# Weights fetched in column halves, eight PSUM banks for the first expert chunks, and a last stage with more buffers

## The chip, the cores and the metric

The kernel runs as one program on all 8 cores of one Trainium2 chip. Each core works on one of the 8 sequences of the batch and needs nothing from the others. The metric is the device time of the slowest core, in microseconds; lower is better.

## The reference

One transformer layer on x of shape 8 x 4096 x 1024 in float32: attention with a single head of width 1024, a residual and a layer norm, then an expert layer in which each of 64 expert slices picks one token out of every group of 16, again with residual and layer norm. Cut to what is computed:

```
qkv = x @ W_qkv + b_qkv;  q, k, v = split(qkv)
attn = softmax(q @ k.T / 32);  out = (attn @ v) @ W_out + b_out
x = layernorm(x + out)
logits = einsum(groups of 16 tokens, controller)        # 16 tokens x 64 slices
perm   = one-hot of the largest logit over the 16 tokens
sel    = the chosen token's row, for each group and slice
inner  = relu(sel @ f1[slice] + bias);  inter = inner @ f2[slice]
out    = inter handed back to the chosen tokens
x = layernorm(x + out)
```

## The kernel before, in words

Five engines run lists of instructions that Python writes out in order; each engine works through its own list strictly in order and waits on counters of the others. `wait` puts a wait in front of the next instruction of a list, `dma`, `mm`, `act` and `ve` append one instruction. So the order of the code is the order on each engine. All DMA starts from the list of SyncE (SP), ScalarE (ACT) or GpSimd (POOL). PSUM has eight banks, `bank(0)` to `bank(7)`; `bank_free[i]` holds the counter value at which bank i may be written again.

**The head.** Attention is reordered by algebra. AM = Wq Wk^T and W2 = Wv Wo are made first, with 128 matmuls each, then V' = x W2 (512 matmuls), then scores = x AM x^T. All weights and the transposed x come in as float32 in pieces of 512 KB: 16 for AM, 16 for W2, 32 for x, numbered as `feeds`. `feed(j)` (L176) starts the DMA of piece j into one of eight staging slots (slot j % 8, after the cast of piece j-8), and puts the cast to bf16 on VectorE (DVE) for even j and on ScalarE for odd j. `product` (L191) makes one half ("part") of AM or W2: four row blocks times two column halves fill all eight banks, and the sum runs over d = 0 to 7, where step d needs the d-th piece of both weight matrices. `evacuate` copies the eight banks out, four on DVE and four on ACT. Between AM and W2 stand small matmuls with the biases: 64 for `UB` (bank 0), 16 for the row constant `WC` (banks 1 and 2), and 16 for the output constant `CO` (banks 3 and 4) which read all of Wo. The V' loop (L267) makes 32 row blocks of 16 matmuls, each half evacuated by DVE with an addition of `CO`.

**The middle** (from some 217 to some 1230 us) is attention over 64 half rows; the change doesn't touch it.

**The expert stage** gathers chosen tokens and multiplies by f1 (until some 1374 us). Then comes a loop over j (L875): `product2(j, k)` multiplies by f2 into a pair of banks, `product2_out` copies the pair to one of two buffers `INP[j % 2]`, on DVE for even k while j < 3, on ACT otherwise; `swap(j-1)` (L665) is one transposing DVE instruction that needs all eight copies of the chunk before. From j = 3 on `combine(m)` (L687) adds the residual (read back from DRAM by `load_hr` into one of two buffers in `CB`) and hands expert outputs back to the tokens, in bank 4 + m % 4; `stats2`, `rstd2`, `shift2` and `finish2` make the layer norm and write y. A finished second half goes through one of two buffers in `WC` (L740), and SP stores it. Blocks 4(j-3) to 4(j-3)+3 are combined in iteration j, so iterations 16 to 19 hold only the end.

Of the kernel before, what the change touches and what calls it, by code (L numbers as in the profile page):

```python
# [49 lines left out]
def build_nc():  # L50
# [102 lines left out]
    d_id = dma(C, "id", IDT[:], ident_d)  # L153
    d_bo = dma(C, "bo", WC[:], bout_d)
    d_fb = dma(C, "fb", FBT[:], fbias_d)
    d_gl = dma(C, "gl", GLM[:], glmask_d)
    d_cb = dma(GP, "cb", CB[:], ctrl_d)
# [6 lines left out]
    for d in range(NC):
        feeds.append((wkt_d[d * 128:(d + 1) * 128, :], V[:, WK + d * 1024:WK + (d + 1) * 1024]))
        feeds.append((wqt_d[d * 128:(d + 1) * 128, :], V[:, WQ + d * 1024:WQ + (d + 1) * 1024]))
    for d in range(NC):
        feeds.append((wvt_d[d * 128:(d + 1) * 128, :], A[:, WV + d * 1024:WV + (d + 1) * 1024]))
        feeds.append((wo_d[d * 128:(d + 1) * 128, :], A[:, WO + d * 1024:WO + (d + 1) * 1024]))
# [803 lines left out]
```

How the kernel before makes its waits and increments, by code:

```python
    def run(q, e):  # L908
        for kind, a, b in q.ops:
            if kind == "wait":
                e.wait_ge(sems[a], b)
            elif kind == "do":
                a(e)
            elif kind == "mark":
                a(e).then_inc(sems[b], 1)
            else:
                a(e).then_inc(sems[b], 16)
```

## Time and profile before

| | |
|---|---|
| runs of the kernel before | 1607.0, 1606.36 and 1603.36 us, median 1606.36 us |
| the profiled execution | 1608.24 us |
| its span, slowest core (core 1) | 1606.7 us; the eight cores 1596.7 to 1606.7 us |
| PE busy | 1445.1 us, 90% |
| DVE busy / ACT busy | 772.5 us, 48% / 492.5 us, 31% |
| granted TensorE clock, mean | 0.930 of full |
| chain that ended last | PE 80%, DMA 8%, ACT 4%, issue 3%, DVE 3% |

The span runs from the first to the last instruction of a core. The page cuts it into 40 slices of 40 us. PE is at 9 tenths from the third slice to the thirty-first; it is below that in the first two and in seven of the last nine, and the granted clock is at 6 and then 5 tenths in the last six. So the two ends are what is not yet full. Each of the rows below gives a start, a duration, the engine, the line, the operation and in brackets how long the engine had been idle and what released it.

### The profile page before, as it was taken

Reading aid. Unit: us, or ns where it says so; the run is one execution under the profiler, and the core shown is the slowest. Engines: PE = TensorE matmul, PEld = TensorE weight load, DVE = VectorE, ACT = ScalarE, POOL = GpSimd, SP = SyncE. Lnnn points to the kernel's source line nnn. Section 1 sums busy time; section 2 is a strip of 40 time slices with the busy share of each in tenths; the row PEclk is TensorE's granted clock in tenths of the full one; section 3 lists DMA queues with packets and bytes.
Section 4 is the critical chain, followed back from the end, with each engine's and each line's share of the span. In section 5 each row is a group of like instructions: output and inputs, shape, how many; then the busy total and the mean of one; then the engine's idle time right before and its main releaser. Section 6 shows DMA issues by size and latency. Waiting matters only on the chain.

```text
span 1606.7 us, 24471 instructions; the slowest of 8 cores (1596.7 to 1606.7 us)
## 1 busy us (share of the span) xinstructions
PE 1445.1 (90%) x8688; PEld 677.2 (42%) x8688; DVE 772.5 (48%) x1493; ACT 492.5 (31%) x825; POOL 99.7 (6%) x165
## 2 busy tenths in 40 slices
PE   4799999999999999999999999999999799477662
PEld 1344434444444444444444444444444577322110
DVE  1234424435534543453453553543464476776772
ACT  2231012121221222122122212212121577488871
POOL 0000000000000000000000000000010330000111
PEclk9899999999999999999999999999999899665555
DMA  9863013644554463453644554462344845024443
GB/s 275 276 192 122 1 42 64 104 69 86 94 97 73 81 123 65 85 88 69 109 79 73 104 88 71 83 108 53 66 97 95 255 167 159 1 63 135 145 158 125
DMA packets 222247, 170.30 MB, mean 106 GB/s; under 512 B 175664, under 2 KB 192176, under 8 KB 221104
## 3 DMA queue, kind: packets, MB, share of 16 engines
q1 hardware_dynamic: 214096, 134.32, 34.6%
q0 software_dynamic: 7312, 33.82, 10.8%
q8 instruction: 72, 1.18, 0.3%
q10 hardware_dynamic: 720, 0.59, 0.1%
q14 instruction: 47, 0.39, 0.1%
HBM read 118.62 MB, written 41.94 MB: 100 GB/s over the span
## 4 chain that ended last, share of the span: by engine, by line
PE 80%; DMA 8%; ACT 4%; issue 3%; DVE 3%; SPq 1%; ACTq 0%; DVEq 0%; POOL 0%; POOLq 0%
PE ps L127 80%; ACT arenaA L136 3%; DMA ctrlb<-hsp 2%; DMA vw<-wqt 2%; DMA vw<-wo 2%; DVE arenaA L141 1%; DMA arenaA<-arenaA 1%; DMA y<-wcrow 1%; DMA xT<-hsp 1%; SPq L123 1%; DVE bnbuf L147 0%; DVE small L142 0%; ACT wcrow L136 0%; DVE small L145 0%; ACT bnbuf L136 0%
## 5 line engine op out<-in xcount | busy, mean ns | idle before, releaser
L127 PE MATMUL ps<-xT,arenaA 128*128 128x512 bf16 x2560 | 565.8, 380 | 12.3 <-ACT arenaA L136 11.3
L127 PE MATMUL ps<-vw,arenaA 128*128 128x512 bf16 (+1 forms) x3072 | 522.9, 379 | 46.8 <-ACT arenaA L136 23.6
L127 PEld LDWEIGHTS ps<-xT,arenaA 128*128 128x128 bf16 x2560 | 247.6, 98 | 307.4 <-issue 19.2
L127 PEld LDWEIGHTS ps<-vw,arenaA 128*128 128x128 bf16 (+1 forms) x3072 | 228.5, 109 | 329.2 <-issue 87.7
L136 ACT ACTIVATE arenaA<-ps,small 128x1024 bf16<-128x1024 f32 x128 | 141.5, 1110 | 516.7 <-DVE small L143 516.7
L145 DVE TENSOR_REDUCE small<-ps 128x1 f32<-128x512 f32 x256 | 175.6, 686 | 243.9 <-PE ps L127 243.8
L136 ACT ACTIVATE arenaA<-ps 128x512 bf16<-128x512 f32 (+2 forms) x312 | 217.5, 768 | 109.2 <-PE ps L127 103.6
L127 PE MATMUL ps<-arenaA,xT 128*128 128x128 bf16 (+1 forms) x1536 | 190.3, 275 | 14.2 <-ACT arenaA L136 8.5
L144 DVE SCALAR_TENSOR_TENSOR arenaA<-ps,small,arenaA 128x1024 f32<-128x1024 f32 x64 | 82.2, 1284 | 187.0 <-PE ps L133 140.2
L127 PEld LDWEIGHTS ps<-arenaA,xT 128*128 128x128 bf16 x1536 | 111.0, 99 | 93.9 <-issue 28.5
L141 DVE CAST arenaA<-ps 128x512 bf16<-128x512 f32 (+1 forms) x136 | 95.6, 734 | 82.3 <-PE ps L127 81.6
L136 ACT ACTIVATE arenaA<-ps,ubias 128x512 bf16<-128x512 f32 x64 | 44.0, 688 | 158.3 <-PE ps L127 158.3
L142 DVE TENSOR_TENSOR small<-small 128x1 f32<-128x1 f32 (+1 forms) x192 | 35.7, 186 | 87.7 <-ACT small L136 70.6
L136 ACT ACTIVATE bnbuf<-bnbuf,small 128x1 f32<-128x1 f32 (+1 forms) x40 | 11.7, 294 | 213.1 <-DVE bnbuf L148 213.1
L672 DVE STREAM_TRANSPOSE xT<-arenaA 128x4096 f32<-128x4096 f32 x16 | 71.1, 4442 | 6.3 <-ACT arenaA L136 6.3
L127 PE MATMUL ps<-arenaA 128*64 128x256 bf16 (+3 forms) x688 | 66.1, 296 | 7.4 <-ACT arenaA L136 3.0
L142 DVE TENSOR_TENSOR vw<-ps,permC 128x512 bf16<-128x512 f32 x64 | 43.9, 691 | 59.4 <-PE ps L127 59.4
L123 POOL DMA_DIRECT2D hsp<-arenaA x32 | 18.3, 573 | 766.7 <-DVE arenaA L143 745.5
L127 PE MATMUL ps<-ctrlb,identb 128*128 128x512 bf16 x64 | 36.4, 569 | 30.8 <-DMA ctrlb<-hsp 18.7
L147 DVE BATCH_NORM_STATS2 bnbuf<-ps 128x6 f32<-128x512 f32 x64 | 43.8, 690 | 35.5 <-PE ps L127 35.1
L127 PE MATMUL ps<-vw 128*128 128x512 bf16 x128 | 32.4, 412 | 22.0 <-ACT vw L136 22.0
L127 PEld LDWEIGHTS ps<-arenaA 128*64 128x64 bf16 (+1 forms) x688 | 39.7, 111 | 29.0 <-issue 12.8
(55 smaller groups left out, 569.7 us busy)
## 6 DMA issues: line engine op xcount, KB each, us to landing
vw<-xt SPq DMA_DIRECT2D x32, 512.0 KB, 11.1
arenaA<-x SPq DMA_DIRECT2D x32, 512.0 KB, 7.5
f1b<-f POOLq DMA_DIRECT2D x32, 256.0 KB, 6.7
hsp<-arenaA POOLq DMA_DIRECT2D x32, 256.0 KB, 4.3
f2b<-f POOLq DMA_DIRECT2D x32, 256.0 KB, 6.5
arenaA<-f1b SPq DMA_DIRECT2D x32, 256.0 KB, 3.9
vw<-f2b SPq DMA_DIRECT2D x8, 1024.0 KB, 6.6
ctrlb<-hsp SPq DMA_DIRECT2D x64, 128.0 KB, 2.2
```

The lines of the kernel that those rows point to most:

```text
L123: q.ops.append(("dma", lambda e, d=dst, s=src, k=kw: e.dma_start(d, s, **k), chan))
L127: fn = lambda e, o=out, l=lhsT, r=rhs, a=first, z=last, k=kw: e.matmul(o, l, r, start=a, stop=z, **k)
L136: return C.mark(lambda e, o=out, s=src, f=func, k=kw: e.activation(o, s, f, **k))
L141: copy = lambda e, *a, **k: e.tensor_copy(*a, **k)
L142: tt = lambda e, *a, **k: e.tensor_tensor(*a, **k)
L144: stt = lambda e, *a, **k: e.scalar_tensor_tensor(*a, **k)
L145: rmax = lambda e, *a, **k: e.reduce_max(*a, **k)
L147: bns = lambda e, *a, **k: e.bn_stats(*a, **k)
L672: sw_tok[j] = ve(lambda e, *a: e.transpose(*a), dst[:, (j % 2) * 128:(j % 2 + 1) * 128], src)
```

## The change

The diff has three parts, one for each place of the program.

1. **The head.** The left matrix of each product (Wq, Wv) is fetched in column halves: one piece now holds 512 columns of two d-steps, so that the first part of AM needs 12 pieces and not 16; the second halves are pieces 12 to 15. The bias of the output, the controller, the identity and two small tables are fetched by POOL after the cast of piece 16, and not at the start. The output constant `CO` is made after W2. `feed_to(n)` writes the feeds out earlier relative to the copies of the banks, and in the V' loop two pieces per row block.
2. **The first chunks.** While j < 3, `product2` rotates over four pairs of banks instead of two.
3. **The last stage.** The loop ends after j = 16. Blocks 56 to 63 have eight residual buffers and four output buffers of their own, in memory that is free by then; blocks 56 to 59 use banks 0 to 3; and the rest is written out in an order by hand.

```
+    for right, left, r_at, l_at, arena in ((wkt_d, wqt_d, WK, WQ, V), (wo_d, wvt_d, WO, WV, A)):
+        for k in range(4):
+            for d in (2 * k, 2 * k + 1):
+                feeds.append(rows(right, d, 0, 1024, arena[:, r_at + d * 1024:r_at + (d + 1) * 1024]))
+            feeds.append(halves(left, k, 0, l_at, arena))
+        for k in range(4):
+            feeds.append(halves(left, k, 1, l_at, arena))
...
-            T.wait(fed[first_feed + 2 * d], fed[first_feed + 2 * d + 1])
+            T.wait(fed[first_feed + d // 2 * 3 + d % 2], fed[first_feed + (12 + d // 2 if part else d // 2 * 3 + 2)])
...
+    fed_n = [0]
+    feed_to(13)
     am_done = evacuate(list(product(AM, wq, wk, 0, 0)))
-    for j in range(16, 24):
-        feed(j)
+    feed_to(22)
+    GP.wait(fed[16])
+    d_bo = dma(GP, "bo", BO, bout_d)
+    d_cb = dma(GP, "cb", CB[:], ctrl_d)
+    d_id = dma(GP, "id", IDT[:], ident_d)
...
     am_done += evacuate(list(product(AM, wq, wk, 0, 1)))
+    feed_to(26)
...
+    feed_to(28)
+    w2_done = evacuate(list(product(W2, wv, wo, 16, 0)))
+    feed_to(34)
+    w2_done += evacuate(list(product(W2, wv, wo, 16, 1)))
+    feed_to(40)
...
+        if t < 12:
+            feed_to(40 + 2 * (t + 1))
...
+    def made_in(j, k):
+        return (k % (4 if j < 3 else 2)) * 2
...
-        b, dq, b0 = j // 4, j % 4, (k % 2) * 2
+        b, dq, b0 = j // 4, j % 4, made_in(j, k)
...
+    def summed_in(m):
+        return m % 4 if 56 <= m < 60 else 4 + m % 4
...
-        SP.wait(lgm_tok[NT - 1], co_tok[m - 2] if m >= 2 else None)
+        SP.wait(lgm_tok[NT - 1], sw_tok[15] if m >= 56 else co_tok[m - 2] if m >= 2 else None)
...
-        if m + 2 < 64:
+        if m + 2 < 56:
             load_hr(m + 2)
...
+            if m >= 56:
+                second = A[:, i * 1024:(i + 1) * 1024].bitcast(F32)
+                C.wait(sh_tok[t // 4], sw_tok[14])
...
-    for j in range(20):
+    for j in range(17):
...
-            if k == 2 and turned:
+            if k == 2 and j > 0:
                 swap(j - 1)
+                if j == 16:
+                    for m in range(56, 64):
+                        load_hr(m)
...
+    for m in range(56, 60):
+        combine(m)
+    for m in range(52, 56):
+        finish2(m)
+    for m in range(60, 64):
+        combine(m)
+    for m in range(56, 60):
+        stats2(m)
+    rstd2(6)
+    stats2(60)
+    stats2(61)
+    shift2(6)
+    for m in (56, 57):
+        finish2(m)
+    stats2(62)
+    stats2(63)
+    rstd2(7)
+    for m in (58, 59):
+        finish2(m)
+    shift2(7)
+    for m in range(60, 64):
+        finish2(m)
```

Three places of the order that this writes. The first is DVE in the head, from the copies of the second part of AM to the first matmuls of V'. `arenaA<-ps` are the copies of banks, `arenaA<-vw` and `xT<-vw` the casts of pieces, `ubias` and `wcrow` the constants UB and WC, `permC` the output constant CO; `st0` to `st6` are the staging slots. Before:

```order
L141 CAST arenaA<-ps 128x512 [waits sT] x4
L141 CAST arenaA<-vw 128x1024 [waits st0]
L141 CAST arenaA<-vw 128x1024 [waits st2]
L141 CAST arenaA<-vw 128x1024 [waits st4]
L141 CAST arenaA<-vw 128x1024 [waits st6]
L141 COPY ubias<-ps 128x8 [waits sT]
L142 TENSOR_TENSOR permC<-ps,wcrow 128x1024 [waits sT,bo]
L141 COPY wcrow<-ps 128x1024 [waits sV]
L141 CAST arenaA<-ps 128x512 [waits sT] x4
L141 CAST xT<-vw 128x1024 [waits st0]
```

And with the change, from the same copies on:

```order
L142 CAST arenaA<-ps 128x512 [waits sT] x4
L142 CAST arenaA<-vw 128x1024 [waits st6]
L142 CAST arenaA<-vw 128x2x512 [waits st0]
L142 COPY ubias<-ps 128x8 [waits sT]
L142 COPY wcrow<-ps 128x1024 [waits sT]
L142 CAST arenaA<-vw 128x1024 [waits st2]
L142 CAST arenaA<-ps 128x512 [waits sT] x4
L142 CAST arenaA<-vw 128x2x512 [waits st4]
L142 CAST arenaA<-vw 128x2x512 [waits st6]
L142 CAST xT<-vw 128x1024 [waits st0]
```

Two casts (pieces 22 and 24) stand ahead of the constants where four stood, CO is gone from here, and the first cast that the second part of W2 needs (piece 28, the one on `st4`) stands behind the four copies of the first part.

The second place is PE at the end of W2. Before, the output constant (`ps<-arenaA,bcolsb`) stands ahead of W2 and waits for the last pieces:

```order
L127 MATMUL ps<-vw,bcolsb 128x512 x16
L127 MATMUL ps<-arenaA,bcolsb 128x512 [waits sC,sV]
L127 MATMUL ps<-arenaA,bcolsb 128x512 x15
L127 MATMUL ps<-arenaA 128x512 [waits sV] x2
L127 MATMUL ps<-arenaA 128x512 x62
```

With the change it stands behind W2 and ahead of V' (`ps<-arenaA,xT`):

```order
L128 MATMUL ps<-arenaA 128x512 [waits sV]
L128 MATMUL ps<-arenaA 128x512 x15
L128 MATMUL ps<-arenaA 128x512 [waits sC]
L128 MATMUL ps<-arenaA 128x512 x15
L128 MATMUL ps<-arenaA,bcolsb 128x512 [waits sV,sC]
L128 MATMUL ps<-arenaA,bcolsb 128x512 x15
L128 MATMUL ps<-arenaA,xT 128x512 [waits sV,sC]
```

W2 no longer waits for its last piece ahead of its first matmul; its own steps wait for their pieces one by one.

The third place is the end of SP's list, with the residual loads (`ctrlb<-hsp`, or `arenaA<-hsp` for the new buffers) and the stores of y. Before:

```order
L123 DMA ctrlb<-hsp 128x512 [waits sT] x9
L123 DMA y<-wcrow 128x512 [waits sC]
L123 DMA ctrlb<-hsp 128x512 [waits sT]
L123 DMA y<-wcrow 128x512 [waits sC]
L123 DMA ctrlb<-hsp 128x512 [waits sT]
L123 DMA y<-wcrow 128x512 [waits sC] x6
```

With the change:

```order
L124 DMA ctrlb<-hsp 128x512 [waits sT]
L124 DMA arenaA<-hsp 128x512 [waits sV]
L124 DMA arenaA<-hsp 128x512 x7
L124 DMA ctrlb<-hsp 128x512 [waits sT] x2
L124 DMA y<-arenaA 128x512 [waits sC] x8
```

The eight new loads wait for a DVE instruction (the last `swap`), and the loads of blocks 54 and 55 (`ctrlb<-hsp x2`) stand behind them in the same list.

## Rows read from the trace of the kernel before

**Rows 1.** Windows of the head: length, busy time of each engine, granted clock, DMA share, GB/s.
```profile
10.00:15.00 5.00, 3.27 (x8) 1.02 (x8) 0.00 (x0) 1.57 (x2) 0.00 (x0) 1.00 1.07 230
...
35.00:40.00 5.00, 3.27 (x15) 1.42 (x16) 1.60 (x3) 1.89 (x4) 0.00 (x0) 1.00 1.00 338
...
65.00:70.00 5.00, 4.31 (x11) 1.55 (x12) 0.00 (x0) 0.55 (x1) 0.00 (x0) 0.50 0.99 329
...
80.00:85.00 5.00, 5.00 (x25) 2.29 (x24) 0.00 (x0) 0.00 (x0) 0.00 (x0) 1.00 0.00 0
```
**Rows 2.** Timeline of PE in the head: start, duration, instruction, count, idle time before.
```profile
38.61 15.79 PE L127 MATMUL ps<-vw 128*128 128x512 bf16 x72 [1.45 <-ACT vw L136]
54.43 1.74 PE L127 MATMUL ps<-bcolsb,vw 128*128 128x1 bf16 x64
...
65.69 6.38 PE L127 MATMUL ps<-arenaA,bcolsb 128*128 128x512 bf16 x16 [6.04 <-ACT arenaA L136]
...
74.95 29.23 PE L127 MATMUL ps<-arenaA 128*128 128x512 bf16 x127 [2.66 <-DVE wcrow L141]
```
**Rows 3.** Timeline of ACT in the head: casts of pieces 11, 15, 21, 23, 31.
```profile
31.46 1.06 ACT L136 ACTIVATE vw<-vw 128x1024 bf16<-128x1024 f32 x1 [2.57 <-DMA vw<-wqt]
...
37.41 1.06 ACT L136 ACTIVATE vw<-vw 128x1024 bf16<-128x1024 f32 x1 [2.28 <-DMA vw<-wqt]
...
47.05 1.06 ACT L136 ACTIVATE arenaA<-vw 128x1024 bf16<-128x1024 f32 x1 [2.14 <-DMA vw<-wo]
50.86 1.06 ACT L136 ACTIVATE arenaA<-vw 128x1024 bf16<-128x1024 f32 x1 [2.75 <-DMA vw<-wo]
...
64.49 1.06 ACT L136 ACTIVATE arenaA<-vw 128x1024 bf16<-128x1024 f32 x1 [2.83 <-DMA vw<-wo]
```
**Rows 4.** Timeline of DVE in the head: piece 2, four bank copies, constant WC.
```profile
15.43 0.69 DVE L141 CAST vw<-vw 128x1024 bf16<-128x1024 f32 x1 [7.70 <-DMA vw<-wkt]
...
39.09 2.48 DVE L141 CAST arenaA<-ps 128x512 bf16<-128x512 f32 x4 [2.24 <-PE ps L127]
...
73.58 1.23 DVE L141 COPY wcrow<-ps 128x1024 f32<-128x1024 f32 x1
```
**Rows 5.** The chain that ended last, in order of time: V' as one piece.
```profile
105.51 110.68 PE ps L127 x512
```
**Rows 6.** The 32 DMAs of the transposed x: issue to landing.
```profile
DMA to landing us min/median/max: 6.5/11.1/13.8
```
**Rows 7.** Timeline of DVE and ACT in the first expert chunks (j = 0 to 3).
```profile
1375.69 1.22 DVE L141 CAST arenaA<-ps 128x1024 bf16<-128x1024 f32 x1
...
1387.88 4.43 DVE L672 STREAM_TRANSPOSE xT<-arenaA 128x4096 f32<-128x4096 f32 x1
...
1407.78 4.45 DVE L672 STREAM_TRANSPOSE xT<-arenaA 128x4096 f32<-128x4096 f32 x1 [0.32 <-ACT arenaA L136]
1408.41 3.85 ACT L136 ACTIVATE arenaA<-ps 128x1024 bf16<-128x1024 f32 x4 [0.73 <-PE ps L127]
```
**Rows 8.** Timeline of the last stage: last swap, blocks 54, 55 and 63, last copy, last store.
```profile
1557.88 4.45 DVE L672 STREAM_TRANSPOSE xT<-arenaA 128x4096 f32<-128x4096 f32 x1 [0.99 <-ACT arenaA L136]
...
1562.03 0.58 PE L127 MATMUL ps<-ctrlb,identb 128*128 128x512 bf16 x1 [1.30 <-DMA ctrlb<-hsp]
...
1563.09 0.61 PE L127 MATMUL ps<-ctrlb,identb 128*128 128x512 bf16 x1
...
1583.55 0.59 PE L127 MATMUL ps<-ctrlb,identb 128*128 128x512 bf16 x1 [2.51 <-ACT wcrow L136]
...
1592.46 0.78 ACT L136 ACTIVATE wcrow<-ps,bnbuf 128x512 f32<-128x512 f32 x1 [1.66 <-DMA y<-wcrow]
1593.31 0.33 SPq L123 DMA_DIRECT2D y<-wcrow  x1
```
**Rows 9.** A window of the last stores, as in rows 1.
```profile
1590.00:1592.00 2.00, 0.00 (x0) 0.00 (x0) 0.00 (x0) 0.78 (x1) 0.17 (x1) 0.50 1.01 367
```
**Rows 10.** DMA issues on the page: KB each, median us from issue to landing.
```profile
ctrlb<-hsp SPq DMA_DIRECT2D x64, 128.0 KB, 2.2
```

More of the change, by code:

```diff
@@ L115, in build_nc @@
     CO = PC[:, 0:2048].bitcast(F32)
+    BO = PC[:, 2048:4096].bitcast(F32)
     EPS = SM[:, 0:1]
@@ L152, in build_nc, with rows, halves @@
     d_bc = dma(C, "bc", BC[:], bcol_d)
[L153 to L157, printed above, removed]
     t_eps = ve(mset, EPS, 1e-5)
+    C.wait(t_eps)
+    act(SM[:, 1:2], EPS, AF.Identity)
     VE.wait(d_bc)
     t_bcb = ve(copy, BCB[:], BC[:])
-    feeds = []
[L164 to L169, printed above, removed]
+    def rows(src, d, col, width, dst):
+        return (src[d * 128:(d + 1) * 128, col:col + width], dst)
+    def halves(src, k, half, at, arena):
+        return (src[k * 256:(k + 1) * 256, half * 512:half * 512 + 512].rearrange("(t p) c -> p t c", p=128),
+                arena[:, at + k * 2048:at + (k + 1) * 2048].rearrange("p (t c) -> p t c", t=2)[:, :, half * 512:half * 512 + 512])
+    feeds = []
+    for right, left, r_at, l_at, arena in ((wkt_d, wqt_d, WK, WQ, V), (wo_d, wvt_d, WO, WV, A)):
[5 more added lines that the diff above has]
+            feeds.append(halves(left, k, 1, l_at, arena))
     for b in range(4):
         for c in range(NC):
-            feeds.append((xt_d[c * 128:(c + 1) * 128, b * 1024:(b + 1) * 1024],
-                          B[:, c * S + b * 1024:c * S + (b + 1) * 1024]))
+            feeds.append(rows(xt_d, c, b * 1024, 1024, B[:, c * S + b * 1024:c * S + (b + 1) * 1024]))
     fed = [None] * len(feeds)
@@ L178, in feed @@
         slot = STF[:, (j % 8) * 1024:(j % 8 + 1) * 1024]
+        if len(dst.shape) == 3:
+            slot = slot.rearrange("p (t c) -> p t c", t=2)
         if j >= 8:
@@ L242, in build_nc @@
                       wq(d)[:, h * 512:(h + 1) * 512], d == 0, d == NC - 1, mark=(d == NC - 1))
-    T.wait(bank_free[3], bank_free[4], fed[17], fed[19], fed[21], fed[23], fed[25], fed[27], fed[29], fed[31])
+    VE.wait(t_u)
+    t_ub = ve(copy, UB[:], bank(0)[:, 0:8])
+    VE.wait(t_wc)
+    t_wcs = ve(copy, WC[:], PS[:, 512:3 * 512])
+    bank_free[0], bank_free[1], bank_free[2] = t_ub, t_wcs, t_wcs
+    feed_to(28)
[3 more added lines that the diff above has]
+    feed_to(40)
+    T.wait(bank_free[0], bank_free[1])
     for h in range(2):
         for d in range(NC):
-            t_co = mm(bank(3 + h), BCB[:, 16 + d:17 + d].broadcast_to([128, 128]),
+            t_co = mm(bank(h), BCB[:, 16 + d:17 + d].broadcast_to([128, 128]),
                       wo(d)[:, h * 512:(h + 1) * 512], d == 0, d == NC - 1, mark=(d == NC - 1))
-    VE.wait(t_u)
-    t_ub = ve(copy, UB[:], bank(0)[:, 0:8])
     VE.wait(t_co, d_bo)
-    t_co2 = ve(tt, CO, PS[:, 3 * 512:5 * 512], WC[:], ALU.add)
-    VE.wait(t_wc, t_co2)
-    t_wcs = ve(copy, WC[:], PS[:, 512:3 * 512])
-    bank_free[0], bank_free[1], bank_free[2] = t_ub, t_wcs, t_wcs
-    bank_free[3], bank_free[4] = t_co2, t_co2
-    w2_done = evacuate(list(product(W2, wv, wo, 16, 0)))
-    for j in range(32, 40):
-        feed(j)
-    w2_done += evacuate(list(product(W2, wv, wo, 16, 1)))
-    for j in range(40, 48):
-        feed(j)
+    t_co2 = ve(tt, CO, PS[:, 0:1024], BO, ALU.add)
+    bank_free[0], bank_free[1] = t_co2, t_co2
     T.wait(*w2_done)
@@ L270, in build_nc @@
             T.wait(*[fed[32 + b * 8 + c] for c in range(NC)])
-            if b in (1, 2):
-                for j in range(40 + b * 8, 48 + b * 8):
-                    feed(j)
+        if t < 12:
+            feed_to(40 + 2 * (t + 1))
         if t == 16:
@@ L282, in build_nc @@
                           c == 0, c == NC - 1, mark=(c == NC - 1))
-            VE.wait(done)
+            VE.wait(done, t_wc)
             bank_free[bk] = ve(tt, V[:, t * 1024 + h * 512:t * 1024 + (h + 1) * 512],
@@ L703, in stats2 @@
         VE.wait(co_tok[m], ag_tok[t - 8] if t >= 8 else None)
-        st_tok[m] = ve(bns, BN[:, o:o + 6], bank(4 + m % 4))
+        st_tok[m] = ve(bns, BN[:, o:o + 6], bank(summed_in(m)))
         if half:
```

35 lines of the change are left out of this document (19 added, 16 removed).

## The prediction

> **What bounds the kernel now.** I read the page's 40 slices first, then the chain of waits, then windows and timelines of the two ends. The middle is full of matmuls, and no instruction of it is touched. What can be won lies before V' (105.51 us) and behind the expert products (some 1374 us).
>
> In the head, PE starts V' at 105.51, and its 512 matmuls take 110.68 / 512 = 0.2162 us each [rows 5]. AM and W2 are 256 such matmuls, 55.4 us, and the three constants are some 9 us: 64 us of work in 105. The rest is waiting. First for pieces: casts of pieces 23 and 31 begin 50.86 and 64.49 apart, so a piece takes 13.63 / 8 = 1.70 us [rows 3], with the DMA engines full at 329 to 338 GB/s [rows 1]. Then 6.04 us in which the output constant waits for the last piece of Wo [rows 2], though W2 could have begun. And after it the 16 matmuls of the constant cost 6.38 us, 0.40 each, at twice the usual time: the granted clock is at its full 2.4 GHz level from 35 to 40 and at the 1.2 GHz level from 65 to 70, behind the pause [rows 1]. From 80 to 85 nothing is fetched at all [rows 1], since the casts that free the slots stand behind the copies of W2.
>
> In the first chunks DVE is the bound. One copy of a pair takes 1.22 us and one swap 4.43 [rows 7], and with two pairs of banks PE and ACT stand still whenever DVE holds one pair during a swap.
>
> In the last stage blocks run one behind the other through two residual buffers and two output buffers: block 54 starts at 1562.03 and waits for a load, block 63 at 1583.55 and waits for an output buffer, and the last store is issued at 1593.31 [rows 8].
>
> **The head, step by step.** Part one of AM now needs pieces 0 to 11. Piece 11 was cast at 31.46, piece 15 at 37.41 [rows 3]. Besides, 1 MB of bias and controller and three small tables no longer stand ahead of it: at 338 GB/s this is 3.1 us. In the stretch where they were fetched only 230 GB/s flowed with full DMA engines [rows 1], and piece 2 was cast only at 15.43 [rows 4]; if that was their doing and not the start's, another 5 x (1 - 230/338) = 1.6 us for this window and as much for one beside it. So between 3.1 and 6.3 us, below that nothing reason excludes (0, if the start is slow by itself). I take 4: piece 11 at 27.5, cast 1.06, then 16 matmuls at 0.2162 = 3.5, part one ends at 32.0. Before: 38.61 + 8 x 0.2162 = 40.3. Part two needs only four pieces more and the banks; four copies of each engine (2.48 us) [rows 4] follow the last matmuls as they did at 39.09, when PE did not wait. It ends at 32.0 + 64 x 0.2162 + 0.1 = 46.0.
>
> Then comes a wait. ACT has the cast of piece 21 ahead of its copies. The 1 MB that I took from the front is now fetched right behind piece 16, so up to piece 21 the bytes are as before: cast at 47.05 [rows 3], less the 0.9 us that I kept beyond the bytes: 46.1. Cast, and one copy of 0.52: the constants start at 47.8 and take what they took, 65.69 - 6.04 - 54.43 = 5.2 [rows 2]: 53.0. WC is copied in 1.23 [rows 4]: W2 starts at 54.4. If piece 24 is late (52.6 by 1.70 a piece), its cast of 0.69 on DVE still ends before the constants do.
>
> W2, part one: 13.84, ends 68.2. Part two waits for the cast of piece 28, which stands on DVE behind four bank copies. These begin when the first bank is complete, 7 x 0.2162 = 1.5 before the end, and take 2.48, then 0.69: 69.9, a wait of 1.7. Part two ends at 83.7. The output constant: 16 x 0.2162 = 3.5, now at the full clock: 87.2. Its addition on DVE (1.22 before) gives 88.5, and V' starts there. The pieces of x for the first row blocks are in the slots by then: piece 39 is 8 pieces behind 31, so 64.5 + 8 x 1.70 = 78.1 [rows 3]. V' itself stays 110.7. The head gains 105.5 - 88.5 = **17.0 us**. Bounds: 14 (no gain at the front, and W2's first part held up by its pieces) and 20 (6.3 at the front, and no delay by piece 21).
>
> **The first chunks.** With four pairs, DVE never waits: from 1375.69 twelve copies and two swaps, 12 x 1.22 + 2 x 4.43 = 23.5, plus 0.02 between them: swap 2 could start at 1399.4; it did at 1407.78 [rows 7], 8.4 less. ACT's first copy of j = 3 came at 1408.41; now it follows the swap 1 (at 1396.8), one DVE copy (1398.0) and eight matmuls of j = 3 into that pair, some 0.9: 1398.9, 9.5 less. From there ACT sets the pace, as each of its copies stands directly behind another in these rows. I take **8.9**, and 7 to 9.5 as bounds: 7 if PE at the 1.2 GHz level can't follow DVE and ACT at once.
>
> **The last stage.** One step of the change works against it. The loads of blocks 54 and 55 now stand on SP behind eight loads, which wait for the last swap, until 1557.88 + 4.45 = 1562.33 [rows 8]. Ten loads of 0.131 MB at 367 GB/s [rows 9] are 3.6 us, and one takes 2.2 from issue to landing [rows 10]: block 54 starts at 1568.1, where it started at 1562.03. So 6.1 us are lost first. By the Trainium skill (DMA: Bandwidth & Descriptors, Anatomy of one DMA) a DMA costs about 2.0 us plus its bytes over 436 GB/s; this would be 2.0 + 3.0 = 5.0 us, block 54 at 1567.3, and 0.8 us more gained. No run here shows 436.
>
> Then nothing holds blocks 56 to 63: one costs 1563.09 - 1562.03 = 1.06, and block 63 starts at 1568.1 + 9 x 1.06 = 1577.6. Before, ACT's last copy ended 1592.46 + 0.78 - 1583.55 = 9.7 after block 63's start, with two waits for an output buffer in it, the last of 1.66 [rows 8]; without them, but with two copies of blocks 58 and 59 at 0.78 ahead, ACT ends at 1577.6 + 9.7 - 3.3 + 1.6 = 1585.6, 7.6 us earlier. But the 16 stores of blocks 56 to 63, 0.262 MB each, now follow closely. DVE has the statistics of block 61 (complete at 1576.6) ahead of the first of them; with about 2 us for statistics, shift and copy the first store is issued at 1578.6. Then 4.2 MB at 367 GB/s [rows 9] are 11.4 us, with 1.8 for the way (2.2 less the 0.4 of its bytes [rows 10]): the last lands at 1591.8. Before, it was 1593.31 + 1.8 + 0.7 = 1595.8. So the stores set the end: 4.0, of which I take **3.5**, since they will not come without a gap. Bounds: 0 (if block 54 lands 3.5 us later, as its load shares the engines with stores still under way) and 7.6 (ACT's gain, if the stores keep up).
>
> **The sum.** 17.0 + 8.9 + 3.5 = 29.4 us. Against the profiled execution, whose time is its span of 1606.7 and 1.5 around it: 1608.24 - 29.4 = 1578.8. The median of the runs is 1.9 below that execution, so 1577 is forecast. The forecast's own range, with the terms off on both sides, is 1572 to 1583.
>
> **The rivals.**
> A. Only the first part of each gain comes: the front saves nothing, part two of W2 and the last stage give nothing (14 + 7 + 0 = 21): 1585. For it: the head hangs on casts that stand behind bank copies in strict order, so one late piece stops PE. Against: the pieces' rate is steady over 27 us [rows 3].
> B. All of it and more: 20 + 9.5 + 7.6 = 37: 1569. For it: the pause of 6.04 and the slow clock behind it go for certain. Against: the 1 MB is only moved, not dropped.
> C. Slower than before. In V', DVE now has a cast before each row block's additions, and the cast waits for its piece. If SP runs in step with these casts, each row block pays a full landing, 11.1 us [rows 6], and not 16 x 0.2162 = 3.46: 12 blocks x 7.6 = 92, less 13.8 for the eight banks' slack: 78 more, 1606 + 78 - 29 = 1655 with the other gains. It decides at a landing over 4 blocks, 13.8 us, since SP may run eight pieces ahead and that is four blocks. The longest landing was 13.8 and the median 11.1 [rows 6], so it holds narrowly; and those were landings with eight in flight. If DVE stays behind only on the last pieces it costs some us; only in step does it outweigh the gains.
> D. The change doesn't do what it says: pieces in halves have rows of 2 KB in place of 4. If these went at half rate, 16 pieces x 1.7 = 27 us come back: 1604. Against: the stores of y have rows of 2 KB too and go at 367 GB/s [rows 9]. By the Trainium skill (DMA: Bandwidth & Descriptors, Specifications) rows from 512 bytes up run at line rate; then nothing is lost.
>
> **How the numbers follow.** Forecast 0.62, A 0.2, B 0.12, C 0.03, D 0.03. The predicted time is the forecast's, 1577. The range reaches from B's time to just past A's, 1569 to 1587. Runs of this kernel lie within 0.2%, 3 us, of each other, which is what can be told from no change. Faster: the forecast, A, B and half of D, 0.955. Within: the other half of D, 0.015. Slower: C, 0.03.
>
> **What would show it.** V' starting near 88.5 in the changed profile, with no idle time over 3 us on PE after 32, and the output constant in 3.5 us. Copies and swaps on DVE without gaps from the first chunk on, and swap 2 some 24 us behind the first copy. A pause of PE of 6 us or more before block 54, then blocks 1.1 us apart. Wrong would be: a V' that takes more than 111 us, a piece rate over 1.8 us in the head, or the last stores ending within 3 us of ACT's last copy.

## The result and the profile after

The changed kernel is faster, by 1.2%. Its profiled execution took 1585.64 us (span 1584.1, slowest core 5, the eight cores 1576.7 to 1584.1), two more took 1588.28 and 1589.42, and the ratio to the kernel before is 0.9884, with a 95% interval of 0.9859 to 0.991, some 18.6 us less. Two further executions, of 1702.98 and 1768.67 us, had one die at a lower clock, which happens to the kernel before as well, and such executions are left out of every ratio and time below. The forecast was 1577 us, and 29.4 us less. So the direction was right and the gain too small: the ratio puts the changed kernel at 1588.0 us (0.9884 of 1606.68, the median before), 11 us above the forecast and 1 us above the upper end of the range. The two profiled executions differ by 22.6 us, and 1578.8 was forecast for this one, so it came 6.8 us late.

Four points of time show where it went. V' starts; DVE starts swap 2 and swap 15; the span ends. On the slowest core of each trace, in us:

| | V' starts | V' to swap 2 | swap 2 to swap 15 | swap 15 to the end | span |
|---|---|---|---|---|---|
| before (core 1) | 105.51 | 1302.27 | 150.10 | 48.82 | 1606.7 |
| after (core 5) | 96.74 | 1292.86 | 147.71 | 46.79 | 1584.1 |
| saved | 8.8 | 9.4 | 2.4 | 2.0 | 22.6 |
| forecast | 17.0 | 8.9 | | 3.5 | 29.4 |

The chunks gave what was forecast, and a little more; the last stage gave somewhat less. The head gave half.

In the head (core 5), windows as in [rows 1]:

```profile
10.00:15.00 5.00, 3.90 (x11) 1.46 (x12) 1.39 (x2) 1.06 (x1) 0.00 (x0) 1.00 0.99 302
...
35.00:40.00 5.00, 5.00 (x24) 2.25 (x23) 1.25 (x2) 2.11 (x2) 1.93 (x3) 1.00 0.95 309
45.00:50.00 5.00, 4.97 (x80) 2.98 (x79) 3.18 (x5) 2.83 (x5) 0.00 (x0) 1.00 1.08 265
50.00:55.00 5.00, 1.89 (x9) 0.69 (x7) 0.00 (x0) 1.06 (x1) 0.00 (x0) 1.00 0.90 206
55.00:60.00 5.00, 2.44 (x6) 0.83 (x7) 2.60 (x4) 1.06 (x1) 0.00 (x0) 0.55 1.01 344
```

PE in the head, as in [rows 2]:

```profile
27.53 19.11 PE L128 MATMUL ps<-vw 128*128 128x512 bf16 x80 [2.16 <-ACT vw L137]
46.68 1.74 PE L128 MATMUL ps<-bcolsb,vw 128*128 128x1 bf16 x64
48.28 3.61 PE L128 MATMUL ps<-vw,bcolsb 128*128 128x512 bf16 x16
57.02 0.59 PE L128 MATMUL ps<-arenaA 128*128 128x512 bf16 x1 [5.13 <-DVE ubias L142]
58.15 15.81 PE L128 MATMUL ps<-arenaA 128*128 128x512 bf16 x63 [0.54 <-DVE wcrow L142]
76.19 15.55 PE L128 MATMUL ps<-arenaA 128*128 128x512 bf16 x64 [2.23 <-DVE arenaA L142]
91.58 3.62 PE L128 MATMUL ps<-arenaA,bcolsb 128*128 128x512 bf16 x16
96.74 3.61 PE L128 MATMUL ps<-arenaA,xT 128*128 128x512 bf16 x16 [1.55 <-DVE permC L143]
```

ACT, with the casts of pieces 11, 21 and 23, as in [rows 3], and the four bank copies behind piece 21:

```profile
26.33 1.06 ACT L137 ACTIVATE vw<-vw 128x1024 bf16<-128x1024 f32 x1 [3.04 <-DMA vw<-wqt]
...
44.82 1.06 ACT L137 ACTIVATE arenaA<-vw 128x1024 bf16<-128x1024 f32 x1 [3.15 <-DMA vw<-wvt]
45.79 2.04 ACT L137 ACTIVATE arenaA<-ps 128x512 bf16<-128x512 f32 x4
51.06 1.06 ACT L137 ACTIVATE arenaA<-vw 128x1024 bf16<-128x1024 f32 x1 [3.23 <-DMA vw<-wo]
```

And DVE, the engine of [rows 4]: four bank copies, pieces 22 and 24, then the constants.

```profile
45.24 2.48 DVE L142 CAST arenaA<-ps 128x512 bf16<-128x512 f32 x4 [2.67 <-PE ps L128]
48.23 0.69 DVE L142 CAST arenaA<-vw 128x1024 bf16<-128x1024 f32 x1 [0.50 <-DMA vw<-wo]
56.10 0.69 DVE L142 CAST arenaA<-vw 128x1024 bf16<-128x1024 f32 x1 [7.18 <-DMA vw<-wvt]
56.72 0.16 DVE L142 COPY ubias<-ps 128x8 f32<-128x8 f32 x1
56.79 1.22 DVE L142 COPY wcrow<-ps 128x1024 f32<-128x1024 f32 x1
```

Read these together. PE finishes the constants at 48.28 + 3.61 = 51.89 and then stands for 5.13 us, "waiting for `ubias`". But the matmuls of UB have ended at 48.42 and DVE is free from 48.92 on; the copy of UB stands in DVE's list behind the cast of piece 24, and that piece lands only at 56.1, after a stretch in which the DMA engines were 0.90 busy and moved 206 GB/s. Behind the pause the granted clock is 0.55 in the window, so mostly at the 1.2 GHz level, and the 63 matmuls of W2's first part take 15.81, where the same 63 take 13.76 at full speed (core 5 of e_all_late below).

This form of the loss is that of cores 3 and 5 alone. On the other six the late cast that stops PE is the one of piece 21: it began at 46.18 and 44.82 on cores 3 and 5, and at 48.51 to 50.08 on the six. ACT's bank copies stand behind it, PE waits 3.16 to 6.18 us ahead of the constants, and WC takes 5.0 to 6.1 us in place of 3.61. PE of core 7:

```profile
51.01 1.84 PE L128 MATMUL ps<-bcolsb,vw 128*128 128x1 bf16 x64 [6.18 <-ACT arenaA L137]
52.72 5.87 PE L128 MATMUL ps<-vw,bcolsb 128*128 128x512 bf16 x16
```

and its ACT:

```profile
49.22 1.06 ACT L137 ACTIVATE arenaA<-vw 128x1024 bf16<-128x1024 f32 x1 [6.36 <-DMA vw<-wvt]
50.19 2.04 ACT L137 ACTIVATE arenaA<-ps 128x512 bf16<-128x512 f32 x4
```

Piece 24 is late on all eight cores (cast at 56.10 to 57.80), and by either way W2 starts at 57.02 to 58.91.

V' itself is as long as before [rows 5]:

```profile
96.74 110.68 PE ps L128 x512
```

DVE in the first chunks, as in [rows 7]: six copies and swap 0, and the last two copies ahead of swap 2.

```profile
1367.03 6.95 DVE L142 CAST arenaA<-ps 128x1024 bf16<-128x1024 f32 x6
1373.90 4.43 DVE L689 STREAM_TRANSPOSE xT<-arenaA 128x4096 f32<-128x4096 f32 x1
...
1387.10 2.32 DVE L142 CAST arenaA<-ps 128x1024 bf16<-128x1024 f32 x2
1389.60 4.45 DVE L689 STREAM_TRANSPOSE xT<-arenaA 128x4096 f32<-128x4096 f32 x1 [0.17 <-DVE arenaA L142]
```

DVE has no gap from its first copy to swap 2: 22.57 us, where it was 1407.78 - 1375.69 = 32.09.

The last stage, as in [rows 8]: last swap, residual loads, block 54, ACT's copies, stores.

```profile
1537.31 4.45 DVE L689 STREAM_TRANSPOSE xT<-arenaA 128x4096 f32<-128x4096 f32 x1 [0.99 <-ACT arenaA L137]
...
1541.83 3.63 SPq L124 DMA_DIRECT2D arenaA<-hsp  x8
...
1545.55 0.85 SPq L124 DMA_DIRECT2D ctrlb<-hsp  x2
1548.65 0.58 PE L128 MATMUL ps<-ctrlb,identb 128*128 128x512 bf16 x1 [8.32 <-DMA ctrlb<-hsp]
...
1558.95 9.18 SPq L124 DMA_DIRECT2D y<-arenaA  x8
...
1561.54 4.11 ACT L137 ACTIVATE arenaA<-ps,bnbuf 128x512 f32<-128x512 f32 x6
```

And two windows of the stores, as in [rows 9]:

```profile
1570.00:1572.00 2.00, 0.00 (x0) 0.00 (x0) 0.00 (x0) 0.00 (x0) 0.00 (x0) 0.50 0.89 332
1572.00:1574.00 2.00, 0.00 (x0) 0.00 (x0) 0.00 (x0) 0.00 (x0) 0.00 (x0) 0.50 0.04 13
```

ACT is done at 1565.65, the stores flow until 1572. So they set the end, as forecast. SP issues eight of them (the line above) and POOL the other eight.

### The profile page after: what moved, and what is told of

The parts are those of the page before. It is cut to its first block, busy times and chain, and to the rows that moved or that the text cites. A ratio compares the mean times of both kernels' runs of the same rounds, so it can differ in the third digit from the quotient of the medians.

```text
span 1584.1 us, 24496 instructions; the slowest of 8 cores (1576.7 to 1584.1 us)
## 1 busy us (share of the span) xinstructions
PE 1439.6 (91%) x8688; PEld 676.5 (43%) x8688; DVE 771.7 (49%) x1493; ACT 491.7 (31%) x826; POOL 102.5 (6%) x169
## 4 chain that ended last, share of the span: by engine, by line
PE 80%; DMA 8%; ACT 4%; issue 3%; DVE 3%; SPq 1%; ACTq 0%; DVEq 0%; POOL 0%; POOLq 0%
PE ps L128 80%; ACT arenaA L137 3%; DMA ctrlb<-hsp 2%; DMA arenaA<-arenaA 2%; DMA vw<-wvt 1%; DMA vw<-wo 1%; DMA vw<-wqt 1%; DVE arenaA L142 1%; DVE bnbuf L148 1%; DMA xT<-hsp 1%; SPq L124 0%; DVE small L143 0%; DVE xT L689 0%; DVE small L146 0%; DMA y<-wcrow 0%
## 5 line engine op out<-in xcount | busy, mean ns | idle before, releaser
L128 PE MATMUL ps<-xT,arenaA 128*128 128x512 bf16 x2560 | 565.5, 380 | 12.3 <-ACT arenaA L137 11.3
L128 PE MATMUL ps<-ctrlb,identb 128*128 128x512 bf16 x56 | 31.6, 564 | 24.8 <-DMA ctrlb<-hsp 16.0
```

The lines of the kernel that those rows point to most:

```text
L128: fn = lambda e, o=out, l=lhsT, r=rhs, a=first, z=last, k=kw: e.matmul(o, l, r, start=a, stop=z, **k)
```

## The experiments

Two theories stood at the start. **Order**: engines work in order, and two late casts (pieces 21 and 24) stand ahead of copies that PE waits for. **Bytes**: POOL's fetches, now put behind piece 16, push the pieces back, and the head is bound by landings whatever the order. Times of whole kernels differ by little here, and the slowest core is another one from run to run. So the readings go by the means of the eight cores of each trace, in us:

| kernel | V' starts | V' to swap 2 | swap 2 to 15 | swap 15 to end | ratio to before (95%) |
|---|---|---|---|---|---|
| before | 103.24 | 1301.71 | 148.10 | 48.86 | |
| after | 95.58 | 1292.31 | 145.94 | 46.35 | 0.9884 (0.9859 to 0.991) |
| p_head | 94.76 | 1303.50 | 147.00 | 48.41 | 0.9966 (0.9954 to 0.9977) |
| p_banks | 102.11 | 1293.65 | 146.44 | 48.73 | 0.9934 (0.9918 to 0.995) |
| p_last | 102.38 | 1302.77 | 147.63 | 47.03 | 0.9988 (0.9977 to 0.9998) |
| e_all_late | 90.18 | 1292.30 | 145.81 | 46.59 | 0.9856 (0.9839 to 0.9874) |
| e_tables_late | 92.63 | 1292.30 | 146.84 | 46.54 | 0.9875 (0.9852 to 0.9898) |
| e_order24 | 92.86 | 1292.12 | 146.07 | 46.88 | 0.9869 (0.9848 to 0.9889) |
| e_cast28 | 92.14 | 1291.55 | 146.99 | 46.86 | 0.9847 (0.9827 to 0.9866) |
| e_load54 | 95.08 | 1292.29 | 146.56 | 40.71 | 0.9874 (0.9822 to 0.9926) |
| e_mix | 86.08 | 1293.74 | 147.42 | 40.45 | 0.978 (0.9721 to 0.9839) |
| e_mix_early | 87.43 | 1293.56 | 147.81 | 40.60 | 0.9776 (0.9725 to 0.9827) |

Columns whose code is the same differ by up to 2.2 us between kernels; a smaller difference of such means tells nothing. By their ratios the kernels with one edit can't be told from the changed kernel, since the intervals overlap; only the two at the bottom lie below its interval. What a single edit did is read from its trace.

### The three parts alone

p_head is the kernel before with the changes of the head only, p_banks with those of the first chunks (`made_in`), p_last with those of the last stage.

> The first part of the change alone, on the kernel before. In the changed kernel V' begins at 96.7 us where it began at 105.5, so if the parts add up this one is worth 8 to 9 us on the slowest core: ratio 0.9945. Theory (the head fell short of its forecast of 17 us because piece 24 comes late and PE's clock drops behind the pause that this makes): V' starts at 95 to 97 here too, with a pause of about 5 us before W2. Rival (the head was worth 17 and another part took it back): V' starts near 88.5 here, ratio 0.989.

> The second part alone. Swap 2 came 9.4 us sooner after V' in the changed kernel, mean of the eight cores. If this part does that alone, swap 2 starts near 1398.5 on a core whose V' starts at 105, and the ratio is 0.994 (9.4 us). Rival (the loop behind takes some of it back, since the loads of the residual and the stores run in the same loop): ratio 0.996 or more, with the stretch from swap 2 to the last swap longer than the 148.1 us that the eight cores of the kernel before have in the mean.

> The third part alone. In the changed kernel the span from the start of the last swap to the end shrank from 48.9 to 46.4 us in the mean of the eight cores. Theory (block 54 waits behind eight loads, about 7 us, and the stores then end last): 2.5 us, ratio 0.9985, block 54 starts some 7 us after the last swap's end. Rival (the last stage got its gain from starting earlier or later against the stores of the loop): a gain of 0 or of more than 5 us.

Measured by the ratios: -5.5, -10.6 and -1.9 us, together -18.0, and the whole change gave -18.6. So the parts add up, as far as intervals of some 2 us each can tell. The chunks are the largest part. The head moved V' by 8.5 us in the mean, of which the time shows only 5.5: its slowest core (1599.9 us; the mean of the eight spans is 1593.7) was further from the mean than that of before (1606.7; 1601.9).

The ratio of p_head, 0.9966 (0.9954 to 0.9977), is a smaller gain than the 0.9945 expected. V' starts where the theory put it (94.76), but the pause isn't where it was expected: on none of the eight cores does PE wait more than 0.7 us right ahead of W2's first matmul. It waits 1.97 to 6.17 us ahead of the constants, behind the cast of piece 21, and WC then takes 5.6 to 6.5 us. p_last shortened its stage by 1.8 us in the mean (2.5 expected), with the expected ratio.

### POOL's fetches later: all of them, or the tables alone

e_all_late is the changed kernel with POOL's block behind the constants and piece 27:

```
     feed_to(22)
-    GP.wait(fed[16])
-    d_bo = dma(GP, "bo", BO, bout_d)
-    d_cb = ...; d_id = ...; d_fb = ...; d_gl = ...
...
     feed_to(28)
+    GP.wait(fed[27])
+    (the same five fetches)
```

e_tables_late leaves the bias (512 KB, `d_bo`) where it was and moves the other four.

> The changed kernel with POOL's five fetches (bias, controller, identity, two tables) behind the cast of piece 27 instead of piece 16. Theory (these fetches slow the pieces down while they run: 265 and 206 GB/s in the windows from 45 to 55 us against 328 before): piece 24 is cast near 50.5 and not at 56.1, W2 starts near 53.3 without a pause of 5 us and with the full clock, V' at 88 to 90, ratio to the changed kernel 0.995 or some 7 us. Rival 1 (the rate is that of half-width pieces or of eight cores reading at once): piece 24 still at 54 or later, V' within 2 us of 96.7. Rival 2 (the fetches do as much harm in their new place): piece 24 early, but pieces 28 to 39 late, and V' no earlier than 94.

> The changed kernel with only the 0.5 MB bias at its place behind piece 16, and the controller (which is cast in flight), the identity and the two tables behind piece 27. It divides the 5.4 us that moving all five gave V' in the mean of eight cores (95.6 to 90.2). If bytes are what costs, the controller's 0.5 MB and the bias's 0.5 MB are worth the same: V' at 92.9. If the cast in flight and the short rows (tables of 32 to 256 bytes a row) cost more than their bytes, V' at 91.3 or less. If the bias costs most (the piece behind it waits), 94 or more.

V' starts 5.4 us earlier with all of them late, and 2.95 with the tables alone, at 92.63. By bytes 92.9 was expected, so no sign here that the small tables or the cast in flight cost more than their bytes. PE on core 5 of e_all_late:

```profile
53.33 13.76 PE L128 MATMUL ps<-arenaA 128*128 128x512 bf16 x63 [1.26 <-DVE wcrow L142]
69.32 13.97 PE L128 MATMUL ps<-arenaA 128*128 128x512 bf16 x64 [2.23 <-DVE arenaA L142]
...
88.29 7.07 PE L128 MATMUL ps<-arenaA,xT 128*128 128x512 bf16 x32 [1.55 <-DVE permC L143]
```

The pause of 5.13 is gone, W2 starts at 53.3 (54.4 was forecast), its first part is at full speed again, and V' starts at 88.3 (88.5 forecast). This core is the earliest of the eight; the mean is 90.18 and the latest 92.41, since four cores still wait 1.17 to 2.35 us ahead of the constants. Piece 24 is cast at 49.60 to 51.52 on all eight and piece 21 at 43.60 to 46.28. So the fetches are what made both pieces late. What they cost the DMA engines stands in the list of queues. Here are the two large queues of the changed kernel from 38 to 58 us (core 5), with packets, MB and their time as a share of 16 engines. POOL's is q0:

```profile
q1 hardware_dynamic: 1767, 4.54, 73.0%
q0 software_dynamic: 416, 1.10, 26.7%
```

1.10 MB took 0.267 x 20 = 5.3 us of all engines, 4.9 us for an MB; the pieces took 3.2 for an MB. The prediction had taken 3.1 us for the megabyte that it moved. And 256 KB of the 1.10 MB are a sixth fetch (`f1b<-f`), which the prediction had overlooked: it stands next in POOL's list, so the new wait on piece 16 moved it as well.

### Order: the cast of piece 24 behind the constants

```
-    feed_to(26)
+    feed_to(24)
```

> The changed kernel with the casts of pieces 24 and 25 behind the copies of the constants UB and WC on DVE and ACT, not ahead of them; nothing is fetched at another time. Theory (W2 waits only since the copies stand behind the cast of piece 24; W2 itself needs that piece 7 us after its start): the pause of 5.1 us before W2 goes on the slowest core and with it the slow clock behind it, V' starts 4 to 6 us sooner than the 95.6 us that the changed kernel has in the mean of eight cores, ratio to the kernel before 0.985. Rival (the late pieces are the bound wherever they are waited for): W2 starts at 53 to 54 but stops at its fifth or seventh step for piece 24 or 27, and V' starts within 2 us of 95.6.

V' came 2.7 us earlier in the mean, less than the 4 to 6 expected, and not on all cores: four start V' at 89.4 to 91.4, the other four (0, 2, 4, 5) at 94.7 to 96.8. PE of core 0, one of the late ones:

```profile
50.55 1.84 PE L128 MATMUL ps<-bcolsb,vw 128*128 128x1 bf16 x64 [4.40 <-ACT arenaA L137]
52.26 5.95 PE L128 MATMUL ps<-vw,bcolsb 128*128 128x512 bf16 x16
```

and its ACT:

```profile
48.76 1.06 ACT L137 ACTIVATE arenaA<-vw 128x1024 bf16<-128x1024 f32 x1 [5.16 <-DMA vw<-wvt]
49.72 2.04 ACT L137 ACTIVATE arenaA<-ps 128x512 bf16<-128x512 f32 x4
```

PE of core 1, one of the early ones:

```profile
47.73 1.74 PE L128 MATMUL ps<-bcolsb,vw 128*128 128x1 bf16 x64
49.33 3.61 PE L128 MATMUL ps<-vw,bcolsb 128*128 128x512 bf16 x16
```

The same fault sits one step earlier, as on six cores of the changed kernel. On core 0 piece 21 was late as well (48.76; 45.94 on core 1), its cast stands on ACT ahead of the bank copies, and the constants wait 4.40 us for bank 1. And the pause costs a second time: the 16 matmuls of WC take 5.95 and not 3.61. The granted clock tells it (core 0):

```profile
52.00:58.00 6.00, 6.00 (x31) 2.42 (x29) 0.36 (x2) 2.11 (x2) 0.00 (x0) 0.58 0.97 310
```

So moving one cast is half a remedy: it can help only where piece 21 came in time. That both belong behind what PE waits for is tried in e_mix_early below.

### The casts of pieces 28 and 29 ahead of W2's bank copies

```
-    feed_to(28)
+    feed_to(30)
```

> The changed kernel with the casts of pieces 28 and 29 ahead of the bank copies of W2's first part. Theory: the wait of 2.23 us between the parts of W2 goes on all cores, and on cores 1, 3 and 5, whose second part took 15.6 us in place of 13.97, the slow clock behind it: V' starts 2.2 to 3.0 us sooner in the mean of eight cores (92.6 to 93.4). Rival (the bank copies are the bound, the cast only rides along): a wait of 1 us or more stays there.

V' came 3.4 us earlier (2.2 to 3.0 expected). The wait of 2.23 us between the parts of W2 is gone on all eight cores, and on seven of them the 127 matmuls take 27.66 (29.93 on core 7), 0.2178 each. In the changed kernel the parts took 29.96 to 34.1 us with the wait in it. On cores 1, 3 and 5 more than the wait went: there the second part had taken 15.55 to 15.66 for 64 matmuls, behind a pause of only 2.23 us. On the other five, with the same pause, it had taken 13.97. That makes some 2.9 of the 3.4 us. Most of the rest is chance, not the edit: in this trace one core (7) waits right ahead of W2, 4.96 us, and has a slow stretch behind it; in the changed kernel two did.

### The loads of blocks 56 to 63 behind those of 54 and 55

```
                 swap(j - 1)
-                if j == 16:
-                    for m in range(56, 64):
-                        load_hr(m)
             if new and 2 <= k <= 5:
                 combine((j - 3) * 4 + k - 2)
+            if j == 16 and k == 3:
+                for m in range(56, 64):
+                    load_hr(m)
```

`combine(53)` issues the load of block 55, so only after it do the eight loads, with their wait for the last swap, enter SP's list.

> The changed kernel with the loads of blocks 54 and 55 ahead of the eight loads that wait for the last swap. Theory (blocks 54 to 63 run 7 us late only because of that order): block 54 starts before the last swap ends, and since the stores run at the full DMA rate behind it, the end comes 5 to 7 us sooner: from the start of the last swap to the end 40 to 41.5 us in the mean of eight cores, where the changed kernel has 46.35. Rival (the eight loads themselves are what blocks 56 to 63 wait for, and they can't start before the swap ends): blocks 56 and on start at 1541.76 + 2.5 to 3 us, some 6 us sooner than now all the same; if it is instead the stores, the gain is under 2 us.

From swap 15 to the end it is 40.71 us, 5.6 less than in the changed kernel, as the theory expected. The ratio, 0.9874, hardly shows it: one of the four executions took 1599.82 us, the others 1580.31 to 1583.68. Core 3:

```profile
1537.69 4.45 DVE L689 STREAM_TRANSPOSE xT<-arenaA 128x4096 f32<-128x4096 f32 x1 [0.99 <-ACT arenaA L137]
...
1541.66 0.59 PE L128 MATMUL ps<-ctrlb,identb 128*128 128x512 bf16 x1 [1.12 <-DMA ctrlb<-hsp]
...
1542.21 4.70 SPq L124 DMA_DIRECT2D arenaA<-hsp  x8
```

Block 54 starts 4.0 us behind the start of swap 15, where it was 11.3 in the changed kernel. Of these 7.3 us 5.6 (in the mean) reach the end; blocks 56 on now wait 1.2 us for their own loads.

### All four edits together, with POOL late and with POOL early

e_mix has the loads of e_load54, POOL's fetches of e_all_late, and this order:

```
-    feed_to(22)
+    feed_to(20)
...
-    feed_to(26)
+    feed_to(22)
...
     feed_to(28)
+    (POOL's wait for fed[27] and its five fetches)
+    feed_to(30)
```

e_mix_early is the same with POOL's fetches where the change put them, behind piece 16. These two tell order from bytes.

> Four edits of the changed kernel together: POOL's five fetches behind the cast of piece 27 instead of piece 16; the casts of pieces 20 and 21 issued behind the AM product's second bank copies, and those of pieces 22 to 25 behind the copies of the constants; the casts of pieces 28 and 29 ahead of W2's first bank copies; the eight fetches of blocks 56 to 63 behind the combine of block 53. Theory (the pause ahead of W2 is in-order engines behind late casts and copies, and W2's parts run at 27.66 us where no pause is between them): W2's first product from 53 to 54.5 us on all eight cores, W2 in one piece of 27.7, V' at 86 to 88.5 us (mean; 95.58 in the changed kernel, 90.18 with the late fetches alone, 92.14 with the early casts alone), end minus swap 15 at 40.5 to 41.5 us (46.35), so 1567 to 1573 us of device time, ratio to before 0.976 to 0.980. Rival (the landings set the pace of the head: with the pauses gone W2's second part, or V', waits for its pieces): waits of 1 us or more for landings of pieces 29 to 39 inside W2 or V', V' start at 89 or later, or V' longer than 110.68 us, and 1574 us or more.

> As e_mix, but POOL's five fetches stay behind the cast of piece 16, as in the changed kernel. Theory of order (the fetches' bytes only delay pieces 22 to 24 by some 3 us, and that costs nothing once no bank copy is behind their casts): W2's first product at 53.5 to 55 us on all cores, V' at 86.5 to 89 us, within 1.5 us of e_mix. Theory of bytes (1 MB of fetches ahead of the pieces costs its transfer time whatever the order): pieces 24 to 28 are still late for W2, waits of 2 us or more ahead of or inside W2's first part, V' at 90 to 92 us, 3 to 5 us behind e_mix.

V' starts at 86.08 and 87.43 us, both inside what the theory of order expected; the fetches' place is worth 1.35 us once no copy stands behind a late cast, and 5.4 us when one does. In e_mix_early piece 24 is cast about as late as in the changed kernel (55.01 to 57.38), and PE has no idle time over 0.1 us right ahead of the constants or of W2 on any core of either kernel. Bytes as the bound would have put e_mix_early at 90 to 92. PE of core 4 of e_mix:

```profile
52.57 27.66 PE L128 MATMUL ps<-arenaA 128*128 128x512 bf16 x127 [1.26 <-DVE wcrow L142]
80.06 3.62 PE L128 MATMUL ps<-arenaA,bcolsb 128*128 128x512 bf16 x16
```

The end came as expected too (40.45 and 40.60). Both kernels beat both the kernel before (by 2.2%, intervals 1.6 to 2.8%) and the changed one: executions took 1573.4 to 1581.5 us, against 1585.6 to 1589.4. The expected 1567 to 1573 was missed by a few us all the same, and two signs of the rival came true, a longer V' and a time above 1574; but PE doesn't wait for pieces in V' there, it runs at a lower clock, which is told last.

## Why the prediction came out as it did

**The front was right.** Piece 11 was cast at 26.33, where it was 31.46 [rows 3]: 5.1 us earlier, and 4.1 in the mean of the eight cores; 4 were taken, 3.1 to 6.3 were the bounds. With six fetches gone from the front, the engines moved 302 GB/s from 10 to 15 us, not 230 [rows 1]. AM's second part ended at 46.6 (46.0 forecast), the constants at 51.9 (53.0; on this core and on core 3 alone).

**The step that failed** is the price of the fetches behind piece 16: "up to piece 21 the bytes are as before", with the cast of 21 at 46.1, and "If piece 24 is late (52.6 by 1.70 a piece), its cast of 0.69 on DVE still ends before the constants do". Both orders had been seen, ACT's copies behind the cast of 21 and UB and WC behind two casts on DVE; but the landings were priced at the rate of [rows 3], as if what POOL fetches there cost the pieces nothing. The first sentence held on cores 3 and 5 (46.18 and 44.82). On the other six piece 21 was cast at 48.51 to 50.08. The second failed on all eight: the cast of 24 began at 56.10 to 57.80, and W2 started at 57.0 to 58.9, on core 5 in full at 58.15 and not at 54.4: 3.7 us. From piece 21 to 27 a piece took (61.25 - 44.82) / 6 = 2.7 us on core 5, so the sign "a piece rate over 1.8 us in the head" came true, and so did the idle time of PE over 3 us after 32. e_all_late took away the fetches and got these back; the two kernels with the new order took away what stands behind the casts and got them back as well. Both are needed for the loss, and either suffices as remedy.

**What followed from it** was not in the sum at all: the clock. On core 5 W2's first part took 15.81 us (2.0 more than forecast) and the second, to the start of the constant, 15.39 (1.6 more), each behind a pause. The wait for piece 28 was 2.23 where 1.7 was forecast (0.5), and constant and addition took 5.16 where 4.8 was (0.4). With the 3.7 of W2's start this is the distance from 88.5 to 96.74. On the six cores that waited ahead of the constants the slow stretch fell into WC, 1.4 to 2.5 us, and W2's first part was at full speed. The prediction had read a slow clock behind the pause of 6.04 us in the kernel before [rows 1, 2] and used it as a gain, but gave its own pauses none.

**A reading of one core.** 105.51 us [rows 5] was the latest V' but not the usual one: the mean of the eight cores was 103.24. In the mean the change gave 7.7 us in the head, and e_mix, with all the pauses away, 17.2. So the 17.0 of the forecast was there to be had, but not by this change: e_mix also takes away the wait for piece 28, of which the forecast had kept 1.7 us.

**The first chunks: right.** Swap 2 came 9.4 us earlier in relation to V' (8.9 forecast, bounds 7 to 9.5) and swap 15 another 2.4; the prediction had ACT 1.1 us further ahead than DVE. p_banks alone shows 8.1 and 1.7 in the mean, 9.7 together. The second figure of each pair is no larger than what such columns differ by anyway.

**The last stage: mechanism right, size a little off.** Block 54 waited for SP's list as said (8.32 us idle). It started 11.34 us behind the start of swap 15; before, it was 4.15 [rows 8]: 7.2 lost, 6.1 forecast. Behind it blocks 54 to 59 ran 1.06 to 1.09 apart, as forecast, at a granted clock of 0.50; from 1554 on it was 1.00, which the prediction didn't have, and the last blocks ran 0.66 apart. ACT ended at 1565.65, 17.0 us behind block 54's start (17.5 forecast), and the stores flowed 6 us more. From 1564 to 1572 they came at 332 to 377 GB/s (367 taken). Instead of 3.5 it gave 2.0 on the slowest core and 2.5 in the mean; 1.1 of the difference is block 54. The prediction had 3.6 us for the bytes of ten loads and 2.2 to land, 5.8 behind the last swap's end; it was 6.9. Block 54's load is the ninth in the list, and SP puts out one in 0.45 us (eight in 3.63), so it was issued at 1545.55, 3.8 us behind the swap's end, and PE started 3.1 us later. In the stretch from 1541.8 to 1548.5 the DMA engines were 0.62 busy. So the first term had about the right size for another reason, SP's issuing rather than the bytes, and most of the 1.1 is the way to the landing, 2.9 us in the median of the two loads (2.2 in [rows 10]). Why these took longer wasn't tried. The Trainium skill (DMA: Bandwidth & Descriptors, Anatomy of one DMA) gives 2.0 us plus bytes over 436 GB/s for one DMA issued by GpSimd. The prediction's use of it for ten loads from SP, 5.0 us, is not what the section states, and the measured 6.9 speaks against that sum here.

**The rivals.** A (only the first part of each gain, 1585 us) is nearest to the time, but by luck in part: its case was a late piece that stops PE, and that is what happened, but its sum had nothing from the front and the last stage, and the front and the chunks gave all of theirs. B, all of it and more, didn't come. C needed V' in step with its landings: V' took 110.68 us as before. D needed halves of rows to be slow: windows with halves among the pieces show 302 and 344 GB/s, and in e_all_late, with the halves as they are, V' starts 5.4 us sooner.

## What to carry to other kernels

When a fetch is moved, it must be charged where it goes at least at what it saved where it was (here 4.1 us at the front in the mean, and 5.4 us of V's start behind piece 16), and everything behind it in the issuing list goes along. In a list that an engine works off in order, nothing that may land late should stand ahead of a copy that another engine waits for: with the copies first, the same fetches in the same place cost 1.35 us. A pause of PE must be priced with the slow stretch behind it, which here cost about half as much again as the wait (2.3 us behind 4.40 on core 0 of e_order24, 2.0 behind 5.13 on core 5 of the changed kernel). And one core is not the kernel: on the slowest core the loss sat at piece 24, on six others at piece 21, and an edit for the one left four cores as they were.
